# Two transformer layers on one core: dense work to the end, contexts by pairs of heads, whole-height spreading of routing weights

## The chip, the cores and the metric

The kernel runs on one core of one Trainium2 chip. The metric is the device time of one execution in microseconds (us), less is better.

## The reference, cut to what matters

Two layers over x of shape (4, 512, 128), all in float32. Layer 0 adds to x an attention across channels (16 heads) and a mixture of 64 experts with a shared one; layer 1 adds a sparse windowed attention and a dense two-matrix network. This is what the change touches (cut, names shortened):

```
# layer 0, experts: rw is (tokens, 64), the eight chosen weights of each token
expert_out = vmap(lambda g, u, d: (silu(x @ g.T) * (x @ u.T)) @ d.T)(Wg, Wu, Wd)
routed = einsum('eth,te->th', expert_out, rw)

# layer 1, attention: 8 heads of 16 channels, a window of 64 positions
q = relu(einsum('btd,nde->btne', x, enc_q)); v = relu(einsum('btd,nde->btne', x, enc_v))
sig = mean(q, time) + 0.5 * mean(q[:, ::8], time)
metric = softplus(base + 0.1 * (gelu(sig @ w1 + b1) @ w2 + b2))
dist = sqrt(sum((q_window - q)**2 * metric) + 1e-8)      # causal window
w = exp(-dist) of the 32 nearest, divided by their sum
context = sum_k w[k] * v[k]
out = (q * (context + gate * 0.1 * heb)) @ decoder

# layer 1, dense: two ternary matrices
r = relu(x @ Wfc'.T); y = r*r @ Wproj'.T
```

## The kernel before, in words

The four batches (b = 0 to 3) are worked through one after the other. `uses()` assigns eight PSUM banks to uses in order; each engine has parts written as generators, and `ORDER` gives for each engine a string of letters that says which part makes its next step. `weave` plays that string, so the order of the work on each of the five engines is fixed by hand or by a planner outside the file. Each engine runs its instructions in that order; semaphores carry the waits (`filled`, `emptied`, `own`).

**Experts.** The 64 experts and the shared one are cut into 46 tiles of 128 hidden rows for each batch, 184 in all. For a tile TensorE does six fp32r matmuls of 128x512 (`experts()`: high and low halves of weights and tokens into banks G and U), ScalarE the SiLU, VectorE the product with U, VectorE or GpSimd in turn the product with the routing weights `Rb`, and TensorE the down projection (`downs()`), which gathers all 46 tiles of a batch in bank A. ScalarE copies bank A to `mo` at the end of the batch. At most five tiles (`RING`) are under way.

**Routing.** `route(b)` on all engines makes the routing weights, turned into `RW`, and `spread(b, k)` (four for each batch) copies them by one matmul with the selection matrix `sel` to the rows of tile form: lhsT and rhs are rows 32k to 32k+31 of `sel` and `RW`. In the opening, batch 0's transposed tokens go bank X, `xT` (ScalarE), `xH` (ScalarE), `xL` (GpSimd), and the first expert matmul waits for `xL`.

**Layer 1.** `head(b)` (letter h) follows when bank A of the batch is copied: normalisation, the encodings `kp` and `v`, the metric (one column: `met`), the operands of the distances. `vt` is stored to DRAM (`vscratch`), and for each of eight groups g of 64 queries SyncE loads overlapping windows `vw` of 79 rows by four (`windows`, line 409 through `load`); `vw` has two buffers, so the load of group g waits until the context matmuls of group g-2 are done. `distances` (d), `near` (n: square root and exponential on ScalarE), `choose` (k: the 32 nearest by MAX8 and MATCH_REPLACE8 on VectorE), `weights` (q, GpSimd), `turns` (t: transposes `turn`, then the contexts `ctx`, after every second group `dec`), `gather` (g, VectorE) and `adds` (p, GpSimd) follow for each group.

A context is four matmuls of 79x128 by 79x128: every head's values with every head's weights. VectorE multiplies the 128x512 result with the block mask `bd` into `wT`; GpSimd adds the eight blocks in three steps into `cT` (semaphore `added`), adds `hf` and multiplies with `kp` after every second group. For the last group VectorE does all of this.

**Dense part.** `dense(b)` (f) works in four steps i: `ff1` (four matmuls of 128x128x128), ScalarE ReLU and square into `PR`, `ff2` (four matmuls), and VectorE adds the 128x128 result to x. Batch 0's and 1's steps run during the experts of batches 2 and 3, three of batch 2's during the experts of batch 3, and the last of batch 2 and batch 3's own after the last expert. Both `ff1` and `ff2` use bank X0.

The SyncE order is: stores of v and eight window loads for each batch, the output of batch b-1 near batch b's v, and in batch 3 the four outputs of 128 rows between the last window loads.

Helpers stand for most lines: L507 is every matmul (`mm`), L516 the first transposes, L767 the `turn` transposes, L797/L801/L805 VectorE operations, L1280 ScalarE's `activation`, L1285 the load of the logarithm table, L1523 GpSimd's `tensor_tensor`, L409 every DMA. A float32 matmul shows as two instructions in the trace.

Of the kernel before, what the change touches and what calls it, by code (L numbers as in the profile page):

```python
# [12 lines left out]
NT = T // 128  # L13
# [15 lines left out]
LNEXP = "natural_log_exp_and_others"  # L29
TAKEN = 0.0  # L30
# [9 lines left out]
        "vvvvvvvvvsvvvvvvvvvsvvvvvvvvvvsvvvvvsvsvvss",  # L40
    "pe":
        "yyeeyeeemaeemeeeeeaeeeaeayeasessasammmememeeememmmeeeemaueaeeauemmeeaeeeummueyeeyemmyemeeeeeemmmeemm"
        "eeeeememeeeeemmmeeemmeeeeeeemyeemmmseemseemeeemmeseeeeeemmmeeeeemmmseemeeemeeemehyeyeeemmmyeeememhee"
        "mhheeheeheehmehememeemeemmemeeemeeeheheemmmdeeeedmymdamaedamdeeeadtaeeeteeameeammeeemtdmemeeetmdeeee"
        "meeemmeteetmataetataeesesefmmfmteemtfteeeememeeftfeefmmfeetemmfeesmteemseymhtmteeeeeeteeytmeemeytemh"
        "mhmemeeheemmeeeeeehhmheeememhmeeeeeymmmeeeehaemheaedeedemaedeaedadeaatdtmmmmemdteemeemdteeememeemaee"
        "etameeetaeametmmeeeemtseetsefmmfemeeeeefmmemteetmeetemfmfmtfteeeeeefeeefmmteeehestmtmseatmtmameeeamt"
        "aeheeaeeheeahmehmeameemhmheeeeehmmmemeeehaeeeemmmeheeaedeeedeeedemmdedmeeemmtmeadteedeeeetemtmmmdmee"
        "eaemmeeteteetfmmemeetmfeteeeeeememfmfteeeetefteemtetmeefmmmmtmmhtfttfthfhthfhhfhhfffhhfddddfdddttttd"
        "tttttttttttttttt",  # L50
    "dve":
        "cyyyyyyyyyyycyyyelyyyeayeyeyyyyyeylaecyyyeyyayyamammyleemeyaaemeaueuluueuuuamuuuemeemleaemeyyylyemey"
        "emyyyeyylyyyemeemeyyyyyemelyeymeyemleemyeyyyelmeemyeyemleemeemleeeeelmhhemheyhyhhemlyeyyyemyyheoehmh"
        "elehyymyeyelyymyyyeyeyhheemeymhlyemeemlyoakakkokkkkeokkeeakkgakmlaekeemkkkemkklaegmeeamkeeagklkkgkke"
        "amaekkgmkkekyfglyyemekegkekkfyeymfelkmemkkgkfkeegkkeemlhhhgheemelemgyyhhygyyeylyyyyoemeyhyemyeyelmye"
        "hhyyyyyeyememeelhyhmahelehmeaeomkkkkoeakkkakkaokkklgkkeemkkakaekememlageemeklgemkekakkkkemaegekkkmlk"
        "kfeemegeemlgemkekkfgkemlkkgekfekkeefkmelgehmhhhgaeghhaemlgeemaeemhaaoelehhmeaemlahhaeemhelemheemeelm"
        "okkkoeekkkkkkkkeomelkeegkkkmkkmgekaeemlkemgkeakkkemlgkkkeemekekfgklekefmmgekekgkklegmkkemekkkgfhkhhh"
        "gfhhghogfhhfhhfhhokkkokfkkkkkkkkkgokgkkkkkkkkggkkkkgkkkgkkkgkkkgkkkkgkkgggg",
    "act":  # L60
        "xxyxyyexcxeexecxxeeexxaayxsxssyaseeexexexaeexxaaxeeuxexexueuyxexyexexeexxexxeexexxeexexxeeexxeexyexs"
        "xesxeyxexexsxexeexexxesxmexeeexxeyxeyxhexxeexhehxehheexxhxhexxexeeexxexhekxxkenkxeexnkynnknanxkneake"
        "kxgeexxeaexexnnxgxexneexexeeaxxgnanagxeexsesxfeexgfexxyexexfexgefxexesxesmxygeexxexexgyheexxhhexhxee"
# [1681 lines left out]
```

## Time and profile before

| What | us |
|---|---|
| time before, median of three runs | 772.04 (766.23 to 772.14) |
| the profiled execution's own time | 761.87 |
| its span | 760.1 |
| PE busy (matmuls) | 690.4 (91%) |
| VectorE busy | 608.9 (80%) |
| ScalarE busy | 424.2 (56%) |
| GpSimd busy | 423.1 (56%) |

PE is TensorE's matmuls, PEld its weight loads, DVE is VectorE, ACT ScalarE, POOL GpSimd, SPq SyncE's queue. "128\*64" behind a matmul is rows by columns of the weights. Idle time in brackets is the engine's own wait before the row, and what ended it.

### The profile page before, as it was taken

The numbers are of one execution on the slowest core, as the hardware profiler recorded it, in microseconds if no ns is written. First come the engines' busy times: TensorE is split into PE (matmuls) and PEld (weight loads), VectorE is DVE, ScalarE is ACT, GpSimd is POOL, SyncE is SP. The second block draws the span as 40 slices with busy tenths as digits, with TensorE's granted clock in tenths as the row PEclk, the third lists the DMA queues.
The fourth block names the chain that finished last, engine by engine and source line by source line (L and its number), as shares of the span: only waits on it lengthen the run. The fifth ranks groups of instructions, "written<-read, shape, count | busy, mean of one in ns | idle before, by whom it ended". The sixth has DMA issues, their size and how long they took to land.

```text
span 760.1 us, 11266 instructions
## 1 busy us (share of the span) xinstructions
PE 690.4 (91%) x3208; PEld 468.9 (62%) x3208; DVE 608.9 (80%) x2520; ACT 424.2 (56%) x763; POOL 423.1 (56%) x515
## 2 busy tenths in 40 slices
PE   2999999999999899999999899999999999788533
PEld 2656765666656577776555676766566677566433
DVE  3898697659979889989769897975858999759973
ACT  4654543657557665564866665456758564377200
POOL 2165456454656775685628677565745666613540
PEclk9989999999999999999999999999999999997555
DMA  9930000000000000001000000001000000010000
GB/s 285 362 80 1 2 0 0 2 1 16 17 1 5 6 13 18 11 4 34 14 1 6 10 8 15 14 5 31 17 1 2 19 11 13 13 40 11 20 26 17
DMA packets 25722, 21.90 MB, mean 29 GB/s; under 512 B 1920, under 2 KB 23596, under 8 KB 25148
## 3 DMA queue, kind: packets, MB, share of 16 engines
q1 hardware_dynamic: 25660, 21.18, 9.4%
q8 instruction: 26, 0.43, 0.2%
q14 instruction: 36, 0.29, 0.1%
HBM read 18.95 MB, written 2.23 MB: 28 GB/s over the span
## 4 chain that ended last, share of the span: by engine, by line
PE 60%; DVE 21%; ACT 6%; DMA 4%; issue 4%; POOL 3%; SPq 1%; DVEq 0%; POOLq 0%; ACTq 0%
PE bank_X L507 19%; PE bank_U L507 14%; PE bank_A L507 13%; PE bank_G L507 13%; DVE S L797 4%; DVE Wk L1214 4%; DMA vw<-vscratch 4%; DVE m L1211 3%; SPq L409 1%; ACT L1285 1%; PE bank_X L767 1%; DVE Wlo L797 1%; ACT L1280 1%; PE bank_X L516 1%; POOL S L1523 1%
## 5 line engine op out<-in xcount | busy, mean ns | idle before, releaser
L507 PE MATMUL bank_A<-S,WdT 128*128 128x512 f32 x368 | 183.2, 602 | 3.1 <-DVE S L797 1.9
L1523 POOL TENSOR_TENSOR Wlo<-Wgu,Whi 128x256 fp32r<-128x256 f32 x138 | 109.3, 797 | 120.8 <-ACT Whi L1280 120.0
L797 DVE TENSOR_TENSOR S<-S,bank_U 128x512 f32<-128x512 f32 x184 | 123.7, 680 | 52.2 <-PE bank_U L507 30.7
L1280 ACT ACTIVATE S<-bank_G 128x512 f32<-128x512 f32 x184 | 107.8, 595 | 95.4 <-PE bank_G L507 89.0
L1523 POOL TENSOR_TENSOR S<-S,Rb 128x512 f32<-128x512 f32 x88 | 119.1, 1355 | 50.2 <-DVE S L797 49.8
L1280 ACT ACTIVATE Whi<-Wgu 128x256 fp32r<-128x256 f32 x184 | 74.2, 413 | 70.8 <-PE bank_U L507 62.2
L507 PE MATMUL bank_G<-xH,Whi 128*128 128x512 f32 x184 | 93.2, 506 | 2.4 <-ACT S L1280 1.2
L507 PE MATMUL bank_U<-xH,Whi 128*128 128x512 f32 x184 | 91.6, 498 | 3.5 <-DVE S L797 3.5
L507 PEld LDWEIGHTS bank_A<-S,WdT 128*128 128x128 f32 x368 | 66.0, 191 | 45.0 <-issue 26.8
L1214 DVE MATCH_REPLACE8 Wk<-m,Wk 128x79 f32<-128x79 f32 x384 | 82.0, 225 | 0.0
L797 DVE TENSOR_TENSOR S<-S,Rb 128x512 f32<-128x512 f32 x88 | 77.4, 881 | 1.8
L507 PE MATMUL bank_G<-xH,Wlo 128*128 128x512 f32 x184 | 73.1, 397 | 0.0
L507 PE MATMUL bank_G<-xL,Whi 128*128 128x512 f32 x184 | 73.0, 397 | 0.0
L507 PE MATMUL bank_U<-xL,Whi 128*128 128x512 f32 x184 | 73.0, 397 | 0.0
L507 PE MATMUL bank_U<-xH,Wlo 128*128 128x512 f32 x184 | 72.9, 396 | 0.0
L1211 DVE MAX8 m<-Wk 128x8 f32<-128x79 f32 x384 | 63.4, 227 | 0.0
L1523 POOL TENSOR_TENSOR wT<-wT 128x256 f32<-128x256 f32 (+1 forms) x62 | 38.3, 618 | 44.6 <-DVE wT L797 42.0
L507 PEld LDWEIGHTS bank_G<-xH,Whi 128*128 128x128 f32 x184 | 34.9, 190 | 26.0 <-issue 14.8
L1280 ACT ACT_TABLE_LOAD x36 | 46.2, 1283 | 4.4 <-PE bank_A L507 2.9
L507 PEld LDWEIGHTS bank_U<-xH,Whi 128*128 128x128 f32 x184 | 34.9, 190 | 22.3 <-issue 10.1
L507 PEld LDWEIGHTS bank_G<-xL,Whi 128*128 128x128 f32 x184 | 35.0, 190 | 13.4 <-issue 8.8
L1523 POOL TENSOR_TENSOR rr<-kp,cst 128x512 f32<-128x512 f32 x16 | 18.9, 1182 | 43.3 <-PE bank_X L507 30.9
(235 smaller groups left out, 1312.6 us busy)
## 6 DMA issues: line engine op xcount, KB each, us to landing
vw<-vscratch SPq DMA_DIRECT2D x32, 158.0 KB
Wgu<-in_Wgu SPq DMA_DIRECT2D x2, 2048.0 KB, 15.4
xs<-in_x SPq DMA_DIRECT2D x4, 256.0 KB, 7.0
wqk<-in_w_qkv SPq DMA_DIRECT2D x1, 1024.0 KB, 7.6
Wgu<-in_Wgu SPq DMA_DIRECT2D x1, 1024.0 KB, 9.4
vscratch<-mo SPq DMA_DIRECT2D x4, 256.0 KB
out<-xs SPq DMA_DIRECT2D x3, 256.0 KB, 2.3
Wgu<-in_Wgu SPq DMA_DIRECT2D x1, 512.0 KB, 5.4
```

Of the source, the lines that this page charges most:

```text
L409: engine.dma_start(dst, src).then_inc(sems(name), 16)
L507: return engine.matmul(dst, lhsT, rhs, start=start, stop=stop)
L516: p = engine.transpose(t[0:rows, 128 * i:128 * i + 128], src3[:, i, :], ident)
L767: p = engine.transpose(t[0:WK, 128 * i:128 * i + 128], Wk[s][:, i, :], ident)
L797: return engine.tensor_tensor(dst, a, b, op)
L1211: top[i] = own(engine.max(w8[:, i, 8 * r:8 * r + 8], v[:, i, :]))
L1214: p = engine.match_replace(wk[:, i, :], w8[:, i, 8 * r:8 * r + 8], v[:, i, :], TAKEN)
L1280: return engine.activation(dst, src, f, bias=bias, scale=scale, accum_out=acc)
L1285: engine.preload_act_table_set(LNEXP)
L1523: return engine.tensor_tensor(dst, a, b, op)
```

## The change

- `spread`: `sel` becomes four matrices of 128x128, each zero outside its 32 rows (made by VectorE from a new constant `quarter`), and each spread is one matmul over all 128 rows.
- Contexts: each of the four matmuls of a group becomes four of 79x32 by 79x32, one for each pair of heads, into 32 partitions of 32 columns. VectorE takes the diagonal halves by two `scalar_tensor_tensor` operations with the per-partition masks `even` and `odd`, adding `hf` on the way, into `cT`. GpSimd's three additions and the addition of `hf` go; its product with `kp` stays.
- Dense: all of it in the order strings stands after batch 2's experts; only batch 0's first `ff1` is ahead of the last expert. `ff2` goes to bank A (free after the last `mo`), four tiles to a bank, one VectorE addition of 128x512 for each batch in place of four. The output store of a batch waits for that; the stores of batches 0, 1 and 2 stand between batch 3's window loads. `yT` has buffers of its own for batches 0 and 1.
- Metric: `w1` is scaled beforehand (`w1s`), the two means are added by accumulating matmuls; ScalarE takes the absolute value; the chain behind the logarithm has two operations instead of six. For batch 3 the GELU table and the logarithm table are loaded ahead of their use.
- Opening: the logarithm table is loaded first; batch 0's `xH` is read straight from PSUM, and VectorE makes `xL` (and the copy `xT`) from PSUM; the first expert matmul may stand ahead of the gate's.
- All five order strings are new.

The diff, without the order strings and cut to the core:

```diff
-        sel = sb("sel", [128, 128], FR)
+        sel = sb("sel", [128, 4, 128], FR)
...
         for i in range(NT):
             add("X0", "ff1", b, i)
-            add("X0", "ff2", b, i)
+        add("A", "ff2", b)
...
-                sp.wait_ge(empty(bank("ff2", b, j)), nth("ff2", b, j) + 1)
+                sp.wait_ge(empty(bank("ff2", b)), nth("ff2", b) + 1)
...
-                mm(t[:, :], sel[32 * k:32 * k + 32, :], RW[32 * k:32 * k + 32, :]).then_inc(
+                mm(t[:, :], sel[:, k, :], RW[:, :]).then_inc(
...
-                    t = fill("ff2", b, i)
+                    if i == 0:
+                        t2 = fill("ff2", b)
+                        pe.wait_ge("mo", B)
...
-                mm(t[0:64, 0:1], w1[:, :], met[:, 3:4]).then_inc(sems("w1"), 1)
+                mm(t[0:64, 0:1], w1s[:, 0, :], met[:, 0:1], True, False)
                 pe.wait_ge("sig", b + 1)
+                mm(t[0:64, 0:1], w1s[:, 1, :], met[:, 1:2], False, True).then_inc(sems("w1"), 1)
...
                     for i in range(GT):
-                        p = mm(t[:, 128 * i:128 * i + 128], vw[s][:, i, :], wT[s][0:WK, 128 * i:128 * i + 128])
+                        for j in range(0, 128, 32):
+                            p = mm(t[j:j + 32, 32 * i:32 * i + 32], vw[s][:, i, j:j + 32],
+                                   wT[s][0:WK, 128 * i + j:128 * i + j + 32])
...
+                if b == 0:
+                    yield
+                    dve.wait_ge("xH", 1)
+                    t = filled("xT", 0)
+                    tt(xLs[0][:, :], t[:, :], xHs[0][:, :].bitcast(F), ALU.subtract).then_inc(sems("xL0"), 1)
+                    emptied(engine.tensor_copy(xTs[0][:, :], t[:, :]), "xT", 0)
...
+                yield
+                dve.wait_ge("ff2_tile", NT * (b + 1))
+                after_adds(b)
+                latest[b] = emptied(tt(x, x, ps("ff2", b)[:, :], ALU.add), "ff2", b)
...
-                    a = emptied(tt(w3, t[:, :].rearrange("p (a n) -> p a n", a=GT),
-                                   bd.unsqueeze(1).to_broadcast([128, GT, 128]), ALU.mult), "ctx", b, g)
+                    dve.wait_ge(*own(stt(c3, t4[:, :, 0, :], K("even"), h3, ALU.mult, ALU.add)))
+                    a = emptied(stt(c3, t4[:, :, 1, :], K("odd"), c3, ALU.mult, ALU.add), "ctx", b, g)
...
+            logarithms()
...
+                if b == B - 1:
+                    table[0] = GELU
+                    engine.preload_act_table_set(GELU)
...
+                a = act(met[:, 5:6], t[:, 8:9], ACT.Abs, bias=mb[:, 2:3], scale=0.1)
...
-                    po.wait_ge(*own(tt(w4[:, :, 0:4, :], w4[:, :, 0:4, :], w4[:, :, 4:8, :], ALU.add)))
-                    po.wait_ge(*own(tt(w4[:, :, 0:2, :], w4[:, :, 0:2, :], w4[:, :, 2:4, :], ALU.add)))
-                    tt(cT[:, t0:t0 + GT * TQ].rearrange("p (a t) -> p a t", a=GT), w4[:, :, 0, :], w4[:, :, 1, :],
-                       ALU.add).then_inc(sems("added"), 1)
```

The orders around the last expert (dn3.45 is the last down projection; ff0.1:2 is `ff2` of batch 0, step 1; letters that repeat are left out). Before, TensorE: ff2.0 to ff2.2 before it, then `dn3.45 mo3 ff2.3:1 turn2.7 ff2.3:2 ctx2.7 y3 ff3.0:1 enc3 v3 ff3.0:2 met ... ff3.3:1 dist3.0 ... dist3.6 turn3.0 ctx3.0 turn3.1 ctx3.1 dist3.7`. After: `ff0.0:1 ... dn3.45 mo3 ff0.0:2 turn2.7 ff0.1:1 ctx2.7 ... y3 ff0.2:2 enc3 ff0.3:1 v3 ... pq3 ff1.2:2 ff1.3:1 dist3.0 ff1.3:2 ff2.0:1 dist3.1 ... dist3.4 turn3.0 dist3.5 ff2.2:2 ctx3.0 dist3.6 ff2.3:1 dist3.7 turn3.1 ff2.3:2 ff3.0:1 ctx3.1 ff3.0:2 ... ff3.2:1 turn3.2 ...`, the last step ff3.3:2 behind ctx3.3. SyncE after (v = window load of batch 3): `v-store, out0, v0, v1, out1, v2, out2, v3, v4, v5, v6, out3.0, out3.1, v7, out3.2, out3.3`; before: `v-store, out2, v0 to v4, out3.0, v5, out3.1, v6, v7, out3.2, out3.3`.

## Rows read from the trace of the kernel before

**Rows 1.** Busy time by stretch: from:to, length, engines busy (count), PEclk, DMA share, GB/s
```profile
100.00:200.00 100.00, 98.71 (x364) 63.50 (x363) 78.25 (x177) 55.44 (x107) 56.47 (x63) 1.00 0.02 5
...
600.00:640.00 40.00, 39.25 (x197) 28.81 (x196) 38.55 (x188) 24.29 (x44) 28.22 (x35) 1.00 0.05 12
...
660.00:680.00 20.00, 15.94 (x97) 12.20 (x95) 11.12 (x35) 11.63 (x21) 5.02 (x8) 0.91 0.14 34
...
700.00:720.00 20.00, 12.15 (x45) 9.68 (x44) 19.63 (x148) 5.84 (x12) 10.42 (x17) 0.50 0.08 20
720.00:740.00 20.00, 6.58 (x27) 5.62 (x26) 14.94 (x110) 1.19 (x2) 8.78 (x16) 0.50 0.10 26
```

**Rows 2.** Timeline of TensorE and SyncE in the tail: start, us, what, idle before
```profile
696.56 2.08 PE L507 MATMUL bank_U<-wT,vw 79*128 79x128 f32 x8 [0.68 <-ACT wT L1280]
...
698.66 0.22 SPq L409 DMA_DIRECT2D vw<-vscratch  x1
...
726.47 2.05 PE L507 MATMUL bank_U<-wT,vw 79*128 79x128 f32 x8 [1.17 <-DMA vw<-vscratch]
735.15 2.05 PE L507 MATMUL bank_U<-wT,vw 79*128 79x128 f32 x8 [5.78 <-DMA vw<-vscratch]
...
752.37 2.05 PE L507 MATMUL bank_U<-wT,vw 79*128 79x128 f32 x8 [5.60 <-DMA vw<-vscratch]
```

**Rows 3.** The chain that ended last, two pieces: start, us, what
```profile
621.13 0.89 PE bank_X L507 x8
...
756.98 0.78 PE bank_X L507 x2
```

**Rows 4.** Timeline of TensorE around one spread
```profile
324.56 1.02 PE L507 MATMUL bank_A<-S,WdT 128*128 128x512 f32 x2
325.51 0.49 PE L507 MATMUL bank_X<-RW,sel 32*128 32x512 f32 x1
325.93 0.50 PE L507 MATMUL bank_U<-xH,Whi 128*128 128x512 f32 x1
326.27 0.39 PE L507 MATMUL bank_U<-xL,Whi 128*128 128x512 f32 x1
326.50 0.40 PE L507 MATMUL bank_U<-xH,Wlo 128*128 128x512 f32 x1
```

**Rows 5.** Timeline of TensorE around layer 0's small matmuls
```profile
280.30 1.09 PE L507 MATMUL bank_X<-wout,z 64*64 64x128 f32 x16
281.32 0.50 PE L507 MATMUL bank_G<-xH,Whi 128*128 128x512 f32 x1
...
529.86 0.40 PE L507 MATMUL bank_U<-xH,Wlo 128*128 128x512 f32 x1
530.18 1.15 PE L507 MATMUL bank_X<-GWk,wqk 128*64 128x64 f32 x32
531.26 1.13 PE L507 MATMUL bank_A<-S,WdT 128*128 128x512 f32 x2
```

**Rows 6.** Groups by line and form: count, busy us, mean ns, idle before
```profile
L1523 POOL TENSOR_TENSOR wT<-wT 128x256 f32<-128x256 f32 x31 | 24.1, 779 | 42.1 <-DVE wT L797 42.0
...
L797 DVE TENSOR_TENSOR wT<-bank_X,cst 128x512 f32<-128x512 f32 x24 | 16.3, 681 | 1.7 <-PE bank_X L507 1.7
```

**Rows 7.** Timeline of the opening
```profile
8.56 1.28 ACT L1285 ACT_TABLE_LOAD   x1
...
14.49 1.97 PE L507 MATMUL bank_X<-gateT,xT 128*128 128x64 f32 x8 [0.69 <-ACT xT L1280]
15.18 1.27 POOL L1523 TENSOR_TENSOR xL<-xT,xH 128x512 fp32r<-128x512 f32 x1 [3.20 <-ACT xH L1280]
...
16.50 0.79 PE L507 MATMUL bank_G<-xH,Whi 128*128 128x512 f32 x1
```

**Rows 8.** Timeline of batch 3's metric on VectorE and ScalarE
```profile
667.40 1.11 DVE L805 SCALAR_TENSOR_TENSOR met<-met 128x1 f32<-128x1 f32 x1
...
672.41 1.28 ACT L1285 ACT_TABLE_LOAD   x1
...
675.21 1.62 DVE L797 TENSOR_TENSOR met<-met 128x1 f32<-128x1 f32 x3 [0.35 <-ACT met L1280]
```

More of the change, by code:

```diff
@@ L29 @@
 LNEXP = "natural_log_exp_and_others"
+GELU = "gelu_and_others"
 TAKEN = 0.0
@@ L75 @@
 for _n, _w in (("ident", 128), ("bd", 128), ("tri", 64), ("neglo", 1), ("ones", 128), ("heads", NH + 128), ("pick", 128),
-               ("eps8", 1), ("sel", 128)):
+               ("eps8", 1), ("even", 1), ("odd", 1), ("sel", 128), ("quarter", 4)):
     CONST[_n] = (_at, _w)
@@ L100, in constants @@
     put("sel", (p[:, None] % 16 == p[None, :] // 8) * 1.0)
+    put("quarter", p[:, None] // 32 == np.arange(4)[None, :])
+    put("even", p[:, None] // HD % 2 == 0)
+    put("odd", p[:, None] // HD % 2 == 1)
     put("eps8", np.full((128, 1), 1e-8))
@@ L191, in uses @@
             add("X0", "sp", b + 1, 1)
-            dense(b - 1)
             add("X0", "sp", b + 1, 2)
-    dense(B - 2)
-    dense(B - 1)
+    for b in range(B):
+        dense(b)
     for b in range(B):
@@ L262, in program @@
         w1 = sb("w1", [128, 64])
+        w1s = sb("w1s", [128, 2, 64])
         b1 = sb("b1", [64, 1])
@@ L310, in program @@
         vt = yn
-        yT = sb("yT", [128, T])
+        yTs = [sb(f"yT{i}", [128, T]) for i in range(2)]
         kp = sb("kp", [128, PADK + T])
@@ L400, in yT_of @@
         def yT_of(b):
-            return xTs[0] if b == B - 2 else yT
+            return yTs[b] if b < 2 else xTs[b % 2]
         def sync_engine(engine):
@@ L668, in dense @@
                     for k in range(4):
-                        p = mm(t[:, 0:128], r[:, 128 * k:128 * k + 128], WpT[:, k, :], k == 0, k == 3)
-                    p.then_inc(sems(full(bank("ff2", b, i))), 1)
+                        p = mm(t2[:, 128 * i:128 * i + 128], r[:, 128 * k:128 * k + 128], WpT[:, k, :], k == 0, k == 3)
+                    p.then_inc(sems("ff2_tile"), 1)
             def routes():
@@ L895, in route @@
                     dve.wait_ge("ld_c", 16)
-                    engine.tensor_copy(sel[:, :], K("sel")).then_inc(sems("sel"), 1)
+                    for k in range(4):
+                        a = ts(sel[:, k, :], K("sel"), K("quarter")[:, k:k + 1], None, ALU.mult)
+                    a.then_inc(sems("sel"), 1)
                 yield
@@ L1099, in setup @@
                 stt(mb[:, 2:3], mb[:, 0:1], 0.1, mb[:, 1:2], ALU.mult, ALU.add).then_inc(sems("mb"), 1)
+                ts(w1s[:, 0, :], w1[:, :], 1.0 / T, None, ALU.mult)
+                ts(w1s[:, 1, :], w1[:, :], 0.5 / (T // 8), None, ALU.mult).then_inc(sems("w1s"), 1)
             def dense(b):
-                x = xb(b)
-                for i in range(NT):
-                    yield
-                    t = filled("ff2", b, i)
-                    after_adds(b)
-                    latest[b] = emptied(tt(x[:, i, :], x[:, i, :], t[:, 0:128], ALU.add), "ff2", b, i)
+                x = xb(b).rearrange("p a c -> p (a c)")
+                yield
+                dve.wait_ge("ff2_tile", NT * (b + 1))
+                after_adds(b)
+                latest[b] = emptied(tt(x, x, ps("ff2", b)[:, :], ALU.add), "ff2", b)
             def head(b):
@@ L1121, in head @@
                 dve.wait_ge(empty(bank("enc", b)), nth("enc", b) + 1)
-                a = own(engine.tensor_reduce(met[:, 1:2], kp[:, PADK::8], AX, ALU.add))
-                dve.wait_ge(*own(ts(met[:, 2:3], met[:, 0:1], 1.0 / T, None, ALU.mult)))
-                stt(met[:, 3:4], met[:, 1:2], 0.5 / (T // 8), met[:, 2:3], ALU.mult, ALU.add).then_inc(sems("sig"), 1)
+                engine.tensor_reduce(met[:, 1:2], kp[:, PADK::8], AX, ALU.add).then_inc(sems("sig"), 1)
                 yield
@@ L1448, in head @@
                 act(hb[:, :], ps("met", b)[0:64, 0:1], ACT.Gelu, bias=b1[:, 0:1]).then_inc(sems("hb"), 1)
+                if b == B - 1:
+                    logarithms()
                 yield
+                t = filled("met", b)
+                sc_.wait_ge("mb", 1)
+                a = act(met[:, 5:6], t[:, 8:9], ACT.Abs, bias=mb[:, 2:3], scale=0.1)
+                a.then_inc(sems("mabs"), 1)
                 sc_.wait_ge("mabs", b + 1)
-                act(met[:, 6:7], met[:, 5:6], ACT.Exp).then_inc(sems("mexp"), 1)
+                act(met[:, 6:7], met[:, 5:6], ACT.Exp, scale=-1.0).then_inc(sems("mexp"), 1)
+                yield
                 sc_.wait_ge(empty(bank("bdq", b)), nth("bdq", b) + 1)
```

164 lines of the change are left out of this document (79 added, 85 removed).

## Prediction, made before the changed kernel was run

> **What bounds the kernel now.** I read first the busy time by stretch [rows 1]. Up to the last expert (some 655 us) the matmuls fill the span: 98.71 of 100 us, and 39.25 of 40 late on. The same rows show the clock at 1.00, that is 2.4 GHz. VectorE is at 78% there, late at 96% (38.55 of 40), GpSimd and ScalarE far below. So this part is as long as TensorE's instruction stream, and what leaves that stream shortens the kernel one to one, as long as VectorE follows. After 660 TensorE is no longer full (15.94 of 20), and from 700 on it is at 12.15, then 6.58 of 20 with the clock at 0.50 (1.2 GHz), while VectorE falls from 19.63 to 14.94.
>
> Next the timeline of the tail [rows 2]. The first context of batch 3 begins at 696.56 and takes 2.08 us; the load of the next window buffer is issued at 698.66, the moment it ends. The following contexts wait for "DMA vw": 726.47, 735.15, 752.37 (a fourth, at 743.87, is alike). They stand 8.5 to 8.7 us apart, and six loads of 8.6 plus 2.1 us for the first to start give 698.66 + 53.7 = 752.4, where the last context stands. So the transfers run end to end, and the tail from 698.66 on is six window loads, whatever the engines do. VectorE idles in that time. The DMA share in [rows 1] is only 0.08 to 0.10, some one and a half engines of 16: these loads are serial, the path is not full.
>
> The kernel is thus a TensorE part, a chain (head of batch 3, some 25 us, and first choice, 16 us), and a DMA part. The sum is made against the profiled execution, 761.87 us with a span of 760.1; the other runs' median, 772.04, is 1.3% more.
>
> **Dense part.** Eight instructions of one `ff1` or `ff2` step take 0.89 us in the chain [rows 3]; a pair 1.8. Before, 11 pairs stand ahead of the last expert (four each of batches 0 and 1, three of 2), after it half a pair: 10.5 x 1.8 = **-18.9 us** in the full part. They move behind it, where TensorE is not full. In the head, 7.5 pairs stand where 4.5 did: 3 x 1.8 = 5.4 us more on an engine that idles 4.1 of 20 us in that stretch [rows 1], so at most some 1.3 us of it should show, and that in return for waits it fills. The other 8.5 pairs stand among the distances and up to the fourth context: at 2.4 GHz 15 us, at 1.2 GHz 31, in the time in which TensorE is idle for the window loads. What covers them is those loads; if it were gone they would cost up to 31. On VectorE 16 additions become four. What is late next is the store of a batch's output: SyncE issues `out1` ahead of window load 2 and `out2` ahead of load 3, and each waits for a whole batch's `ff2`. `out1`'s addition stands ahead of the first choice, so it is in time. `out2`'s stands behind the third choice, some 19 us after the first begins, and load 3 is not needed by the queue until load 2 is through (8.6 us after context 0, at about the same time): taken at 0, up to 6 us if it slips. Three stores of 256 KB now share the DMA engines with the loads. 16 engines carry one, so each adds its sixteenth to the busy one, 16 KB against the 158 KB of 8.6 us: 0.9 us each, and one or two of them fall after context 0: **+0.9**.
>
> **Spreads.** A spread costs more than its matmul, since it is over 32 rows and its neighbours over 128 [rows 4]. Two down projections (0.86) from 324.56 would end at 325.42; the spread begins at 325.51, the next starts 0.42 later and the one after 0.34, where whole-height fp32r matmuls of 512 columns stand 0.23 apart (326.27 to 326.50). Over 128 rows this is 0.23 and no switch: 0.09 + 0.19 + 0.11 = 0.39 saved, by 16: **-6.2 us**. The bounds are 0 and -8. Four makings of `sel` on VectorE instead of one delay the opening by some 0.5 us, behind ScalarE's weight copies.
>
> **Contexts.** This is the cost of the change. A group has now 32 instructions (16 matmuls, two each) of 32 columns by 32 in place of eight of 128, which take 0.89 like a dense step, with the same loads [rows 3]. No row has this form. The nearest is the similarity product, 128 rows by 64 columns, 64 streamed, the two column halves in turn [rows 5]: 32 in 531.26 - 530.18 = 1.08, 0.034 each. Entering a column form costs 0.09 (530.18 against 529.86 + 0.23), leaving it 0.11 as in [rows 4]. So 1.28 against 0.89, +0.39, and 23 groups stand ahead of the last expert: **+9.0 us**. Bounds: half the columns could halve the time (0.54 + 0.2, -3.5 us in all); or each costs what the 64x64 form does [rows 5], 281.32 - 280.30 = 1.02 for 16, 0.064 each: 2.25, +31 us. I take 0.034 because that row has the same full height and column tiles; its neighbour streams 128 columns, which alone explain 0.053.
>
> Behind them VectorE's 0.681 us mask [rows 6] becomes two operations on 128x64, 0.2 to 0.3 each, -0.2 by group; GpSimd loses an addition of 0.779 us [rows 6] and two smaller ones by group. GpSimd is not the bound, so I cost this at nothing in the full part. Only at the very end is it on the path: from the last context's end (754.42) to the last decode, 756.98 [rows 2, 3], six VectorE operations take 2.5 us, and three would take 1.0: **-1.4 us**.
>
> The Trainium skill speaks against this edit in two places. "TensorE: Matmul & The Clock Gate", section "Wait — 56ns, not 53.3ns?", has the sequencer spend about 62 ns on each MATMUL when the array work is shorter than that; by it a group would take some 2.0 us and the edit would cost about 25 us. Its section "Part 3: Packing small matmuls — row/col tiling" lets a weight load run beside a matmul only in another row group, and the four column tiles share all rows. The similarity rows at 0.034 us for a load and a matmul contradict both, so I don't follow them, but they are the first rival.
>
> **Opening.** The table load at 8.56 (1.28 us) goes ahead of the data, and `xT`, `xH`, `xL` become `xH` from PSUM (0.6) and a VectorE subtraction (0.7, against GpSimd's 1.27) [rows 7]: the first expert matmul comes some 2.5 us earlier than 16.50. But the gate's matmuls (1.97) filled that wait, and stand now behind it. I take **-2.0** (bounds -0.5 and -3.5).
>
> **Head, choice.** In the metric a 1.11 us operation beside GpSimd goes, a table load of 1.28 us is made ahead, and four operations after the logarithm go, of which three took 1.62 [rows 8]: 3.5 to 4 us. Against it stand dense steps on ScalarE (1.25 us each) between the GELU, the exponential and the logarithm, and the 1.3 us of TensorE from above. Net **-2.0** (bounds -5 and +6). The first turn of batch 3 stands no longer behind the distances of group 6: **-0.7**.
>
> **Sum.** -18.9 - 6.2 + 9.0 - 2.0 = -18.1 up to the last expert; -2.0 - 0.7 - 1.4 + 0.9 = -3.2 behind it: -21.3. 761.87 - 21.3 = 740.6, a ratio of 0.972, and on the median 772.04 this is **750.5 us**.
>
> **Rivals.**
>
> *Small context matmuls cost more by the piece.* For: no row shows 32x32 tiles, and [rows 5] has 0.064 for 64x64. Against: the 0.034 row, the nearest in height. 23 groups x 32 = 736 pieces, so each 0.01 us above 0.034 costs 7.4 us; from 0.063 the gain is gone. At 0.064 the kernel stands at 772. If each piece costs what a 128-column load and matmul does, 0.112 (0.89 by 8), it is 57 us more: 808. This is the case that ends slower.
>
> *The dense part is given back behind the experts.* The head becomes TensorE's own length, or its ScalarE steps delay the metric; the output store holds SyncE ahead of a window load. For: 15.94 of 20 are already busy, and the clock halves behind 696, which doubles a pair to 3.6 us. Then the head's -2.0 becomes +3.4 and a late load 3 adds 3 to 6: about 760.
>
> *The full part doesn't follow.* VectorE at 96% in 600 to 640 takes over as the bound in the last batch, and half of the dense gain stays off the path: +10, 761. Against it: VectorE's own work shrinks too, and over the whole part it is near 80%.
>
> **Chances.** Forecast 0.68; context pieces at 0.063 or more 0.07 (0.02 of it near no change, 0.05 slower); given back 0.15; doesn't follow 0.10. A measurement of this kernel can tell about 1% from no change. Below 764.3: 0.68, and most of the second and third rivals, 0.86 in all; within 1% 0.09; slower 0.05. The range is 734 to 765: the low end has contexts for nothing, the opening and head at their best; the high end takes in both middle rivals. The low side also holds that the later runs may stand as near the profile as 741.
>
> **What would show it.** After: the spreads 0.23 us before their successor, as 128x512; contexts x32, 1.08 to 1.3 us from start to next; the last down projection some 18 us earlier; GpSimd's `wT` additions gone; contexts of batch 3 still 8.6 us apart waiting for the window DMA, and the stretch from the first context of batch 3 to the end at 61 us (63.5 before, from its start). Wrong would be: contexts of 2 us or more at the full clock; gaps between TensorE's rows in the last batch's experts with VectorE named; window loads further apart than 9 us with an output issue between them; or a head longer than 25 us from `mo` to the first distance.

## The result, and the profile after

| | before | changed |
|---|---|---|
| median of the runs beside each other, four each | 769.65 us | 735.36 us |
| ratio, 95% interval | | 0.957 (0.951 to 0.963) |
| profiled execution | 761.87 us | 739.74 us |
| its span | 760.1 us | 737.9 us |
| last `mo` copy, and the time from it to the end | 653.09, 107.01 | 634.40, 103.50 |

Between the profiled executions it is 22.1 us, between the medians 34. Executions of both kernels gather at two levels that go with the mean granted clock (before some 763 us at 0.947 and some 771 at 0.933, changed some 735 at 0.970 and some 740 at 0.962), so the profiled pair sets before's shorter level against the changed kernel's longer one, and like against like the change is worth 28 us (763 to 735) or 31 (771 to 740). In a later set (`e5_after_again`) it is 740.06 against 763.06, 0.970 (0.968 to 0.971). The argument below is from the profiles.

Busy time of the kernel before, by the stretches between its `mo` copies (one copy a batch; the last row is the tail). Columns as in [rows 1]:

```profile
158.73:326.53 167.80, 165.11 (x782) 110.40 (x780) 146.68 (x617) 103.87 (x188) 104.82 (x125) 1.00 0.04 10
326.53:497.39 170.86, 165.78 (x800) 113.78 (x798) 143.44 (x601) 104.91 (x187) 108.27 (x133) 0.99 0.04 12
497.39:653.09 155.70, 153.69 (x735) 102.54 (x733) 125.56 (x535) 96.42 (x168) 97.34 (x113) 1.00 0.05 12
653.09:760.10 107.01, 64.51 (x326) 51.04 (x326) 75.51 (x486) 39.44 (x77) 36.27 (x58) 0.68 0.08 22
```

The same of the changed kernel:

```profile
16.00:159.20 143.20, 135.36 (x555) 89.53 (x556) 114.18 (x263) 72.11 (x133) 71.93 (x77) 0.96 0.20 66
159.20:321.55 162.35, 157.62 (x877) 101.93 (x876) 138.15 (x584) 102.40 (x187) 92.56 (x103) 1.00 0.04 11
321.55:482.19 160.64, 157.13 (x924) 100.70 (x922) 141.48 (x633) 96.77 (x176) 96.25 (x105) 0.98 0.04 11
482.19:634.40 152.21, 148.70 (x902) 94.93 (x903) 124.65 (x552) 89.45 (x162) 83.43 (x86) 0.99 0.04 12
634.40:737.90 103.50, 65.59 (x732) 54.20 (x731) 71.88 (x470) 49.98 (x97) 19.61 (x25) 0.83 0.10 27
```

The stretches shrink by 5.5, 10.2 and 3.5 us. TensorE's busy time shrinks by 21.1 us in the three, and its idle time grows from 9.8 to 11.8. The first stretch, with all of the opening's edits, is no shorter: the first `mo` copy came at 158.73 and comes at 159.20. Keep this stretch apart in all that follows: a run whose edit isn't in it can still differ from before there by 2 us, with the clock. So each part is also given between its own first and last `mo` copies, which are 494.4 us apart before and 475.2 in the changed kernel (-19.2).

Now the two small matmul forms that the prediction priced. TensorE's timeline of the changed kernel, answering to [rows 4] and [rows 5]:

```profile
145.46 0.39 PE L512 MATMUL bank_G<-xH,Wlo 128*128 128x512 f32 x1
145.69 0.40 PE L512 MATMUL bank_X<-RW,sel 128*128 128x512 f32 x1
145.93 1.02 PE L512 MATMUL bank_A<-S,WdT 128*128 128x512 f32 x2
...
256.71 0.40 PE L512 MATMUL bank_U<-xH,Wlo 128*128 128x512 f32 x1
257.04 0.46 PE L512 MATMUL bank_X<-wT,vw 79*32 79x32 f32 x32
257.43 1.13 PE L512 MATMUL bank_A<-S,WdT 128*128 128x512 f32 x2
```

The spread stands 0.24 from its successor, where 0.23 was forecast. The context group does not: from its start to the next instruction 0.39 us, not 1.08. With 0.10 to enter the form (257.04 against 256.71 + 0.23) and 0.11 to leave it (the down projections behind it show 1.13 where they show 1.02 at 145.93), a group takes 0.6 us where the old one took 0.89 [rows 3]. The new form is cheaper than what it replaces.

TensorE in the tail of the changed kernel, answering to [rows 2]:

```profile
678.25 0.46 PE L512 MATMUL bank_U<-wT,vw 79*32 79x32 f32 x32
...
707.20 0.66 PE L512 MATMUL bank_U<-wT,vw 79*32 79x32 f32 x32 [1.03 <-DMA vw<-vscratch]
715.75 0.66 PE L512 MATMUL bank_U<-wT,vw 79*32 79x32 f32 x32 [5.72 <-DMA vw<-vscratch]
724.25 0.66 PE L512 MATMUL bank_U<-wT,vw 79*32 79x32 f32 x32 [3.74 <-DMA vw<-vscratch]
733.09 0.66 PE L512 MATMUL bank_U<-wT,vw 79*32 79x32 f32 x32 [7.10 <-DMA vw<-vscratch]
```

Still 8.5 us apart, still on the window loads: the tail from the first context on is the same six transfers.

### The profile page after: what moved, and what is told of

Read it like the earlier page. It is cut to its first block, busy times and chain, and to the rows that moved or that the text cites. A ratio compares the mean times of both kernels' runs of the same rounds, so it can differ in the third digit from the quotient of the medians.

```text
span 737.9 us, 12696 instructions
## 1 busy us (share of the span) xinstructions
PE 667.7 (90%) x3984; PEld 443.9 (60%) x3984; DVE 596.5 (81%) x2527; ACT 414.0 (56%) x759; POOL 367.5 (50%) x406
## 4 chain that ended last, share of the span: by engine, by line
PE 48%; DVE 37%; issue 4%; POOL 4%; ACT 3%; DMA 2%; SPq 1%; DVEq 0%; ACTq 0%; POOLq 0%
PE bank_X L512 13%; PE bank_A L512 12%; PE bank_G L512 11%; PE bank_U L512 10%; DVE S L809 9%; DVE Wk L1233 9%; DVE m L1230 6%; DVE GWk L809 2%; DMA vw<-vscratch 2%; SPq L414 1%; DVE rr L809 1%; POOL S L1550 1%; DVE hg L817 1%; DVE Wlo L809 1%; PE bank_X L521 1%
## 5 line engine op out<-in xcount | busy, mean ns | idle before, releaser
L512 PE MATMUL bank_A<-S,WdT 128*128 128x512 f32 x368 | 188.0, 613 | 2.1 <-POOL S L1550 1.2
L1550 POOL TENSOR_TENSOR S<-S,Rb 128x512 f32<-128x512 f32 x88 | 117.4, 1335 | 94.7 <-DVE S L809 94.3
L809 DVE TENSOR_TENSOR S<-S,bank_U 128x512 f32<-128x512 f32 x184 | 124.0, 679 | 43.4 <-PE bank_U L512 27.2
L512 PE MATMUL bank_U<-xH,Whi 128*128 128x512 f32 x184 | 96.2, 523 | 9.1 <-DVE S L809 8.8
L512 PE MATMUL bank_G<-xH,Whi 128*128 128x512 f32 x184 | 98.3, 534 | 3.9 <-POOL Wlo L1550 2.1
L512 PEld LDWEIGHTS bank_U<-xH,Whi 128*128 128x128 f32 x184 | 35.3, 192 | 34.1 <-DVE S L809 17.7
L512 PEld LDWEIGHTS bank_U<-xL,Whi 128*128 128x128 f32 x184 | 35.3, 192 | 14.3 <-issue 10.3
L1550 POOL TENSOR_TENSOR Wk<-Ed,Wk 128x316 f32<-128x316 f32 x31 | 29.5, 953 | 23.4 <-DVE Wk L1233 23.2
L512 PEld LDWEIGHTS bank_G<-xH,Wlo 128*128 128x128 f32 x184 | 35.2, 191 | 8.5
```

The source lines that it names most:

```text
L512: return engine.matmul(dst, lhsT, rhs, start=start, stop=stop)
L809: return engine.tensor_tensor(dst, a, b, op)
L1550: return engine.tensor_tensor(dst, a, b, op)
```

## The experiments

Before's place of the last `mo` copy and the rest of its span are 653.09 and 107.01; the changed kernel's are 634.40 and 103.50.

**Contexts.** First the changed kernel with its context matmuls at the old width:

```diff
-for j in range(0, 128, 32):
-    p = mm(t[j:j+32, 32*i:32*i+32], vw[s][:, i, j:j+32],
-           wT[s][0:WK, 128*i+j:128*i+j+32])
+p = mm(t[:, 128*i:128*i+128], vw[s][:, i, :], wT[s][0:WK, 128*i:128*i+128])
```

> The changed kernel with the four context matmuls of a group at their old width (79x128 by 79x128); VectorE still reads 128 columns of the bank, which are then those of the wrong heads, so the output lacks the right contexts. In the changed kernel's trace 32 pieces of 32 columns start and are done in 0.39 us, with 0.1 us of switching on either side. Theory A (TensorE's stream bounds the part ahead of the last expert): a group costs 0.89 instead of 0.59 us, 23 groups ahead of the last expert give +6.9 us, the last context at the slow clock +1.5: about 743 to 745 against 735.4. Theory B (the form of the matmul is hidden, the edit's gain is in what VectorE and GpSimd no longer do): under +2 us, 735 to 737.

Then the kernel before with the contexts by pairs of heads and nothing else of the change (the short matmuls as above, two VectorE operations on 64 columns, no additions on GpSimd; orders as before without those additions).

> The kernel before with the contexts by pairs of heads alone (matmuls, VectorE's two operations with hf, GpSimd's additions gone), orders otherwise as before. Theory A with the measured 0.59 us a group: -0.30 x 23 = -6.9 us ahead of the last expert and -2.9 us behind the last context, together -9 to -10 (ratio about 0.987). Theory as predicted (0.034 us for a piece): +9 us ahead of the last expert, -1.4 at the end, ratio 1.010. Theory B (the order string decides, small gains are lost again): only the end's -2.9, ratio 0.996.

Measured: e1 741.94 us, 0.971 (0.966 to 0.976) of before. e2 755.21 us, 0.989 (0.983 to 0.994). So the part that was forecast to cost 9 us and give back 1.4 gains 8.8 alone by its ratio, and the rival with pieces of 0.06 us or more is dead. The profile of e2 splits it: the last `mo` copy comes at 649.65 (-3.4), and 102.75 follow (-4.3). The -3.4 has two parts. The first `mo` copy comes 2.4 us late (161.12, with the clock at 0.96 up to there where before had 0.98), though batch 0's experts have no contexts among them and the orders there are before's; between the first and the last copy e2 gains 5.8 us of the 6.9 that theory A had. Three rows of its tail show the 4.3:

```profile
693.50 0.66 PE L506 MATMUL bank_U<-wT,vw 79*32 79x32 f32 x32 [0.68 <-ACT wT L1275]
...
747.47 0.66 PE L506 MATMUL bank_U<-wT,vw 79*32 79x32 f32 x32 [6.77 <-DMA vw<-vscratch]
749.26 0.76 PE L506 MATMUL bank_X<-dec,hg 128*128 128x128 f32 x2 [1.14 <-DVE hg L798]
```

At 1.2 GHz a context is 0.66 us where it was 2.05 [rows 2]. The first one, shorter by 1.4, lets the chain of loads begin 1.4 us sooner; the last is shorter by 1.4; and behind it VectorE's additions are 1.4 shorter, the one item of the three that was priced. First context to last is 53.97 us (693.50 to 747.47), where before had 55.81 [rows 2].

In e1 the reverse was worth less than its rows say. Its groups cost 0.3 us more each, 6.9 over 23, yet its last `mo` copy stands at 635.18, 0.8 behind the changed kernel's (0.1 between the first and the last copy), and beside the control below (0.970) its ratio differs by 0.001. That was the first sign that TensorE's stream does not pass its savings on one to one. It also leaves open what made the gain of e2: e1 puts back TensorE's part of the edit alone, while e2 takes work off VectorE and GpSimd as well.

**Spreads.** The kernel before with `sel` in four masked copies and the spread's matmul over 128 rows:

```diff
-mm(t[:, :], sel[32*k:32*k+32, :], RW[32*k:32*k+32, :])
+mm(t[:, :], sel[:, k, :], RW[:, :])
```

> The kernel before with the spreads over all 128 rows alone. Theory A: 16 x 0.39 = -6.2 us (ratio 0.992). Theory B (the spreads stand where TensorE waits anyway, or VectorE follows late): 0 to -2 us. The opening may lose 0.5 us by the three more makings of sel.

Measured: 764.46 us, 1.002 (0.999 to 1.006): no gain, 6.2 were forecast. The profile:

```profile
159.37:326.58 167.21, 164.25 (x782) 110.66 (x780) 146.60 (x617) 103.84 (x189) 104.83 (x125) 1.00 0.04 10
326.58:499.53 172.95, 170.44 (x799) 117.30 (x798) 146.12 (x601) 104.71 (x186) 107.22 (x133) 0.95 0.04 12
499.53:654.74 155.21, 153.23 (x735) 102.73 (x733) 125.48 (x535) 96.30 (x168) 97.30 (x113) 1.00 0.05 12
```

Four spreads a batch should take 1.6 us out of each stretch. Two stretches are 0.6 and 0.5 us shorter than before's; the one between them lost 2.1, with the clock at 0.95 where before had 0.99. A third of the sum arrived in the two, and one dip of the clock outweighed it. What began that dip isn't in TensorE's rows ahead of it. From 390 on they are those of before within 0.02 us, up to this one, in e3 and then in before:

```profile
403.06 2.00 PE L508 MATMUL bank_X<-mk,rr 128*128 128x79 f32 x8
403.07 1.12 PE L507 MATMUL bank_X<-mk,rr 128*128 128x79 f32 x8
```

From there the clock of e3 is 0.51 and 0.50 up to 418, that of before 1.00. So a run of one profile can't tell a spread's gain in that stretch from the clock, and the spreads stay at 1.1 us shown out of the two others.

**Dense part alone.** The kernel before with the whole dense part behind the last expert, by the changed kernel's code (`ff2` of a batch in one bank, one addition of 512 columns) and its order from the last `mo` copy on:

```diff
-            dense(b - 1)
...
-    dense(B - 2)
-    dense(B - 1)
+    for b in range(B):
+        dense(b)
```

> The kernel before with its dense part alone moved behind the last expert, as the change has it (one addition of 512 columns for a batch; its order behind the last mo copy is the changed kernel's, the rest of the orders is that of before with the dense letters taken out). Theory A (the prediction's pricing: 10.5 pairs at 1.8 us leave TensorE's full stream, hidden behind the metric at the end): 744 to 747 us, ratio 0.973 to 0.979, all of the gain ahead of the last mo copy (653.1 to about 635), tail within 2 us of 107. Rival B (part is given back: with other stages late, TensorE idles in the places the pairs had, and the two levels of the granted clock eat some): 750 to 756 us, ratio 0.983 to 0.991. Rival C (the twelve added pairs lengthen the tail by more than 5 us): mo copies as in A, tail above 112.

> The kernel before with the dense part last, as in the run before with it, but in ScalarE's order behind the last expert the metric's exponential stands behind the first ReLU of the second batch and its logarithm ahead of the next one. There the logarithm stood behind a ReLU, VectorE waited 6.7 us for it and TensorE, idle for 3 us, fell to 1.2 GHz while dense pairs had to run. Theory A (the 13 us that the tail had grown are that order, not the twelve pairs' own time): mo copies as there (160.4, 327.2, 494.8, 649.4), tail 108 to 113 instead of 120.0, ratio to the kernel before 0.995 to 1.000. Rival B (the pairs themselves lengthen the tail): tail 117 or more, ratio 1.005 or more.

Measured: e8 770.69 us, 1.010 (1.008 to 1.012), slower than before. e9 765.58 us, 1.002 (0.999 to 1.005). Ahead of the first `mo` copy the edit changes nothing. What the first order did, in TensorE's and VectorE's timelines of e8:

```profile
674.55 2.05 PE L483 MATMUL bank_A<-WpT,PR 128*128 128x128 f32 x8 [3.07 <-ACT PR L1257]
676.38 1.92 PE L483 MATMUL bank_X<-yT,WfT 128*128 128x128 f32 x8
679.65 2.08 PE L483 MATMUL bank_A<-WpT,PR 128*128 128x128 f32 x8 [1.35 <-ACT PR L1257]
...
679.72 0.55 DVE L775 TENSOR_TENSOR met<-met 128x1 f32<-128x1 f32 x3 [6.69 <-ACT met L1257]
```

TensorE stood 3.07 us, the clock fell to 0.76 in 671 to 676 and 0.50 in the five us after, a dense step then took 1.9 us instead of 0.9, and the metric's logarithm stood behind a ReLU that waited for those steps: VectorE waited 6.69 us. Two operations moved in ScalarE's order gave back 6.3 us (tail 119.96 in e8, 113.67 in e9). The same place in TensorE's timeline of e9:

```profile
676.06 1.16 PE L483 MATMUL bank_A<-WpT,PR 128*128 128x128 f32 x8 [1.82 <-ACT PR L1257]
677.05 1.06 PE L483 MATMUL bank_X<-yT,WfT 128*128 128x128 f32 x8
```

That was half of the tail's growth of 13.0 us, and not all of what theory A claimed (108 to 113): 6.7 us remain. From the `mo` copy to the first distance matmul it is 31.1 us (650.33 to 681.44) where before had 27.2. This is the forecast's 1.3, at 3.9.

The larger miss is ahead of the tail. The last `mo` copy comes at 650.33 instead of 653.09, the first at 161.02 instead of 158.73 (clock 0.96 against 0.98, the same instructions in the same orders). Between them it is 489.3 us instead of 494.4: **5.1 us for eleven pairs priced at 18.9.** The stretches of e9:

```profile
161.02:328.45 167.43, 160.50 (x718) 103.65 (x716) 146.47 (x613) 99.51 (x181) 104.85 (x125) 0.99 0.04 10
328.45:495.62 167.17, 160.16 (x736) 106.68 (x734) 141.31 (x596) 100.75 (x178) 107.27 (x132) 0.98 0.04 10
495.62:650.33 154.71, 149.68 (x687) 96.81 (x685) 126.28 (x534) 92.98 (x162) 98.40 (x114) 1.00 0.04 11
```

64, 64 and 48 instructions left the stream (so batch 0's and 1's dense steps had stood among the experts of batches 1 and 2, not 2 and 3 as the description of the kernel says), at sixteen a pair eleven pairs, and 14.2 us of TensorE's busy time. But its idle time rose from 2.7, 5.1 and 2.0 us to 6.9, 7.0 and 5.0: 9.2 of the 14.2 us became waiting. Of the 4.7 us between 18.9 and 14.2 some may be the clock (0.99 and 0.98 in the first two stretches, 1.00 and 0.99 before); the rest wasn't taken apart.

**Who it waits for.** The next two runs lighten VectorE and GpSimd, whose lateness is the suspect:

```diff
-tt(s[:, :], s[:, :], Rb[k][:, :], ALU.mult)
+tt(s[:, 0:8], s[:, 0:8], Rb[k][:, 0:8], ALU.mult)
```

> The kernel before with the multiplications by the routing weights (22 of 46 products in a batch, on VectorE and GpSimd) cut from 512 columns to 8: this leaves the weighting of the other columns out. It takes some 14 us of VectorE's and more of GpSimd's time out of each batch. Theory A (TensorE's stream is the bound up to the last expert, as the prediction said; idle 4.0, 2.7, 5.1 and 2.0 us): the last mo copy comes at most 4 us earlier (653.1 to 649 or later), ratio 0.994 or more. Rival B (the other engines' lateness is already in that idle time and in the granted clock): 8 us or more earlier.

> The dense part last, mended as in the first of these runs, and the weight multiplications cut to 8 columns as in the second (it leaves the same weighting out). Theory A (with the pairs gone from the stream, products that VectorE and GpSimd deliver late are what TensorE waits for, so that of 20 us of pairs only 3.7 us were gained): the idle time of the three segments falls from 18.0 us to 9 or less, and the last mo copy comes 8 to 15 us ahead of that of the first run (649.4 to 634 to 641), more than twice what the same cut gives the kernel before. Rival B (it is the clock or the order of the banks, and not the load of the other engines): the cut gives what it gives the kernel before, within 3 us.

Measured: e10 755.7 us (six of its ten runs, 748.76 to 758.42), 0.989 (0.984 to 0.993), last `mo` copy at 647.08; e11 746.35 us, 0.974 (0.965 to 0.983), last `mo` copy at 632.26. The profiled execution of e10 took 762.95 us. Its tail is 7.1 us longer than before's, with the clock at 0.62 where before had 0.68, so only what lies ahead of it is used. There the clock is nearly that of before:

```profile
157.93:323.03 165.10, 164.28 (x782) 110.72 (x780) 129.13 (x617) 103.89 (x189) 75.56 (x125) 1.00 0.04 11
323.03:492.87 169.84, 166.43 (x800) 114.30 (x798) 125.61 (x601) 105.09 (x186) 79.55 (x133) 0.98 0.04 12
492.87:647.08 154.21, 152.80 (x735) 102.95 (x733) 111.80 (x537) 96.44 (x168) 68.47 (x113) 1.00 0.05 13
```

The last `mo` copy of e10 is 6.0 us earlier than before's, between the two expectations. That of e11 is 18.1 earlier than e9's, but 6.2 of it are in the first stretch (154.78 against 161.02), where neither has a dense step. Between the first and the last copy the cut gives the kernel before 5.2 us and the kernel with the dense part last 11.8, over twice as much. Read the other way, moving the dense part is worth 5.1 us with the other engines as they are and 11.7 with them lightened. The idle time of TensorE in the three stretches falls from 19.0 us in e9 to 9.5 (2.6, 4.0 and 3.0); theory A had 9 or less. The cut also shortens each tile's way through its buffers, of which there are five (`RING`), and it lightens two engines at once: which of these counts wasn't taken apart. The stretches of e11:

```profile
154.78:315.44 160.66, 158.04 (x718) 103.51 (x716) 127.98 (x613) 99.50 (x180) 75.81 (x125) 1.00 0.04 11
315.44:480.61 165.17, 161.22 (x736) 108.21 (x734) 123.71 (x594) 100.40 (x179) 78.20 (x131) 0.97 0.04 10
480.61:632.26 151.65, 148.69 (x687) 97.35 (x685) 111.23 (x534) 92.85 (x163) 69.85 (x115) 1.00 0.04 11
```

**Both large parts.**

> The kernel before with the dense part last (mended) and the contexts by pairs of heads, the two large parts together; alone, the one brought the last mo copy from 653.1 to 649.4 and the other to 649.7. Theory A (the two gains add up, and the rest of the change's 18.7 us up to there came from its new orders): last mo copy at 645 to 648, ratio to the kernel before 0.984 to 0.990. Rival B (the contexts' part takes work off VectorE's and GpSimd's way, a product of 512 columns and three additions for a group, which is what the dense part's gain needs): more than the sum, last mo copy at 642 or earlier, ratio below 0.981.

Measured: 760.84 us, 0.994 (0.990 to 0.998); last `mo` copy at 643.04, tail 114.76. The gain ahead of the tail is 10.0 us where the two alone make 6.2, between the two expectations. But the first stretch, where none of the three edits has a part, is 2.3, 2.4 and 1.4 us longer than before's in e9, e2 and e12, and the sum of two counts it twice. Between the first and the last `mo` copy e12 gains 11.4 us and the two alone 5.1 and 5.8, 10.9 together: they add up, as theory A had it, and don't help each other. And the head is 34.7 us now (643.04 to 677.73), and by the ratio both parts together give 4.7 us, less than the contexts alone. Some 20 us of the change's gain are in neither, 8.6 ahead of the tail and 11.3 in it. What is left for it are the shorter metric and opening, the spreads and the new orders; these weren't taken apart. The waits of VectorE from 160 to 630 point to the orders. Before:

```profile
DVE S L797 <- ACT S L1280: 18.4, 14, 4.9
```

and in the changed kernel, where e12 still has 17.7:

```profile
DVE S L809 <- ACT S L1293: 6.1, 11, 1.1
```

VectorE's queue stood 18.4 us behind SiLUs that ScalarE had not delivered, and what TensorE wanted from it stood behind them. The new orders take 12 us of that away; VectorE's waits for TensorE's bank U rise from 18.2 to 22.5 in the same time. That these 12 us are the missing gain is argued, not shown: in e11 VectorE waits 20.2 us for the same SiLUs, and its last `mo` copy is earlier than the changed kernel's (632.26 against 634.40), so the length of this wait alone doesn't tell what it costs. No run has the new orders alone.

**Opening and window loads**, with the changed kernel as its own control:

> The changed kernel as it is, on the chip and in the call of the next three, so that they are compared with it and not with runs of another session. Both theories: its ratio to the kernel before lies at 0.961 to 0.969 if the kernel before runs at its quicker level of 762 to 765 us here (735.4 / 763), and at 0.957 only if that one runs at its slower level of 770 to 773 us, as it did in most of its runs beside the first measurement of the change. Then the part of the 34 us that the two profiled spans do not show (22.2) is the level of the kernel before, not the change.

> The changed kernel with two instructions moved forward in VectorE's order of the opening: the product for expert step 0.3 to ahead of the routing comparison, that for 0.4 to ahead of the four MAX8. Theory A (the opening's expected gain was given back by this order, since TensorE stood 2.96 us at 30.4 for the bank that the product for 0.3 frees): the hole closes, the first mo copy comes 2 to 3.5 us earlier (159.2 to some 156.5), the granted clock behind it no longer dips at 31 to 51, ratio to the changed kernel 0.993 to 0.997. Rival B (the hole is only moved: the routing chain ends about 1.3 us later, the spreads and the attention behind it wait instead): within 0.2% of the changed kernel, first mo copy within 0.7 us.

> The changed kernel with window loads of 80 rows instead of 79 (the last row is not used; it is read from a row more in DRAM). Theory A (in the tail the loads of 79 rows run on one DMA engine, 8.6 us each end to end, and set its length): 80 rows go over 16 engines, a load lands 2 to 4 us after its issue, contexts of batch 3 no longer wait for it, and the tail becomes VectorE's choices: 8 to 11 us less, about 726. Theory B (the tail is set by the choices and the chain behind them, the waits for the loads only fill what would be waited for anyway): under 2 us less, 733 to 735.

> The changed kernel with both the windows of 80 rows (as in the run before with them) and the two products moved forward. If the two gains are independent, as one lies in the first 160 us and the other behind the last mo copy at 634: about 730.3 - 2.5 = 728 us, ratio to the changed kernel 0.988 to 0.991. If the early order gives nothing: that of the 80 rows alone, 0.993.

Measured: e5 740.06 us, 0.970 of before (0.968 to 0.971); e6 736.90, 0.966 (0.963 to 0.968); e4 730.31, 0.954 (0.947 to 0.961); e7 728.04, 0.955 (0.952 to 0.957). The opening's gain was real and was spent: the first expert matmul came at 13.81 instead of 16.50 [rows 7], but VectorE's new order ran the routing chain ahead of one product (TensorE's timeline, then VectorE's):

```profile
33.33 0.80 PE L512 MATMUL bank_U<-xH,Whi 128*128 128x512 f32 x1 [2.96 <-DVE S L809]
...
32.59 1.28 DVE L809 TENSOR_TENSOR S<-S,bank_U 128x512 f32<-128x512 f32 x2
```

With the two products moved forward (e6) TensorE's matmuls run on to 32.4. Then it waits 1.67 us for VectorE's `Wlo` (up to 34.03) and 1.70 for its `xn` (up to 36.67), and the clock of 36 to 41 is 0.50:

```profile
31.00:36.00 5.00, 2.30 (x9) 1.05 (x7) 4.86 (x33) 3.76 (x8) 1.01 (x2) 0.92 0.96 350
36.00:41.00 5.00, 4.33 (x11) 2.92 (x12) 4.22 (x15) 0.99 (x3) 0.56 (x1) 0.50 0.92 227
```

So the hole of 2.96 us became two of 3.37 together: it was moved, as the rival said. The first `mo` copy still came 1.7 us earlier than the control's (157.76 against 159.49), less than theory A's 2 and more than the rival's 0.7, and on top of the wider windows nothing can be told (0.955 in e7, 0.954 in e4).

The window loads are the tail. With one row more a window (80 instead of 79; the store wrote one row more and nothing else changed):

```diff
-vw = [sb(f"vw{i}", [WK, GT, 128]) for i in range(2)]
+vw = [sb(f"vw{i}", [WK + 1, GT, 128]) for i in range(2)]
...
-return bass.AP(rows.tensor, rows.offset, [[128, WK], [TQ * 128, GT], [1, 128]])
+return bass.AP(rows.tensor, rows.offset, [[128, WK + 1], [TQ * 128, GT], [1, 128]])
```

the DMA view of 678 to 728 gives a median of 2.4 us from issue to landing, and the last contexts of e4 wait for no load:

```profile
vw<-vscratch SPq DMA_DIRECT2D x6, 160.0 KB, 2.4
```

```profile
706.85 0.66 PE L513 MATMUL bank_U<-wT,vw 79*32 79x32 f32 x32 [0.68 <-ACT wT L1294]
...
723.97 0.66 PE L513 MATMUL bank_U<-wT,vw 79*32 79x32 f32 x32 [0.68 <-ACT wT L1294]
```

Its last `mo` copy is at 634.40 as in the changed kernel, and 94.40 us follow instead of 103.50. VectorE waits for little but itself then (2.9 us from 678 on, 11.8 in the changed kernel), so its choices are what is left. e4 and e7 are the shortest of all these kernels; the wider windows are to be kept.

## Why the prediction was right, and where it was wrong

The forecast was -21.3 us on the profiled execution; it is -22.1. Ahead of the last `mo` copy -18.1 was forecast and -18.7 came; behind it -3.2, and -3.5 came. Almost none of the terms is right by itself. The total holds because a large cost that was not there stands against gains that did not arrive, and that is luck. So is the match to a microsecond: it is with this pair of profiled executions, and like against like, as above, the change is worth 28 to 31 us.

- *"As long as TensorE's instruction stream, and what leaves that stream shortens the kernel one to one, as long as VectorE follows."* This is the step that failed. The condition was named, looked at as a busy share of 78% and 96%, and set aside at a chance of 0.10. A share says nothing of the order: an engine with an in-order queue can be late at each step with a fifth of its time free. Taken alone, between the first and the last `mo` copy, the dense part gave 5.1 of 18.9 us and the spreads 1.1 of 3.1 in the two stretches where the clock is like; with VectorE and GpSimd lightened the dense part gave 11.7. The contexts, which take work off those two engines as well, gave 5.8 of 6.9. The rival "the full part doesn't follow" was the true mechanism of a large part of this, with half of the dense gain lost as it said and more. In the whole change -19.2 came between the copies. Why it gives 7.7 us more than e12 there isn't shown; new orders that let the others follow are the likely reason.
- *Contexts, +9.0.* The mis-sized term. 32 pieces were priced at 0.034 us by the similarity rows, and take 0.39 together, 0.012 each. That is below the lower bound that was given, a half of the similarity's time. On TensorE's stream the term is -6.9 (23 x 0.3; in both traces 22 groups stand ahead of the last down projection, which makes it -6.6), 16 from the forecast; on the kernel before it gave -5.8 between the first and the last `mo` copy. The warning that was cited from the Trainium skill ("TensorE: Matmul & The Clock Gate", section "Wait — 56ns, not 53.3ns?") is out by more: 32 MATMULs and their 32 loads start within 0.39 us, 12 ns for a load and its MATMUL. The section gives its 62 ns for matmuls decoded by the sequencer's software, with the hardware's decoding off; the prediction left this condition out, and no run here shows which of the two was on. Not to follow it was right, on the evidence of rows.
- *Behind the last context, -1.4.* 7.7 us before (752.37 to 760.1), 4.8 now (733.09 to 737.9). The VectorE part is the 1.4 forecast; a context that is 1.4 us shorter at 1.2 GHz was left out, there and at the start of the chain of loads.
- *Spreads, -6.2.* The size on TensorE was right, 0.24 to the successor. It did not arrive alone.
- *Opening, -2.0.* The first expert matmul did come 2.7 us earlier; 2.96 went back at 30.4 behind VectorE's new order. It moved the first `mo` copy by +0.5.
- *Head, -2.0,* and *first turn, -0.7.* The head, to the first distance matmul, went from 27.2 to 26.4 us. It was counted with 7.5 pairs where the order and the trace have 7, so that 2.5 pairs, 4.5 us, came in and not 5.4. They cost 3.9 in e9, not 1.3, and the shorter metric and its order must have gained more than was counted. From the last `mo` copy to the first context it is 43.9 us, where before had 43.5: +0.4 for the -2.7 of the two terms. The tail's total holds by the term before this one. A head longer than 25 us was named as a sign of being wrong; it had been longer in the kernel before, too.
- *Stores, +0.9,* and *six window loads end to end:* right. From the issue of the first load to the last context it was 53.7 us and is 54.3 (678.78 to 733.09). The first context to the end was forecast at 61 us and is 59.65; the loads still set the contexts' places, as the 80-row run shows by taking them away. But "VectorE idles in that time" holds late only: from 700 to 720 it was busy 19.63 of 20 us [rows 1], and so the tail without the loads' waits is 9.1 us shorter and not more.
- For the median 750.5 was forecast and 735.4 came, near the low end of the range, and -34 us where the scaled sum had -21.5.

## What to carry to other kernels

A gain on the fullest engine is worth only what the engines that feed it in order can keep up with (here 5.1 us of 18.9, and 11.7 with less work on them). Their busy share doesn't tell this; take the block out, see how much of it turns into waits, and lighten the others as a test. Compare stretch by stretch, and first one that the edit can't touch: 2 us of difference there are not the edit's. And where a transfer sets the pace, look first at its shape: one row more was worth 9 us of span, about twice the 4.7 us that the two largest parts of the change gave together in e12.

## What the runs showed of the hardware

- Matmuls of 32 columns by 32 in four column tiles, 79 rows deep, start 0.012 us apart on average (32 in the 0.39 us from 257.04), each with its weight load, although all four share the same rows. Changing into and out of the form costs 0.10 and 0.11 us, once for a group of 32. At 1.2 GHz the group took 0.66 us, and the eight of 128 columns 2.05.
- A load of 79 rows takes 8.5 us for 158 KB and one of 80 rows 2.4 us for 160 KB. The Trainium skill's page "DMA: Bandwidth & Descriptors", section "Why a DMA increments its semaphore by 16 and not by 1", splits a transfer over the largest number up to 16 that divides its slowest dimension: 1 for 79 and 16 for 80. The trace agrees: some 19 GB/s over the tail of the changed kernel while loads run, and a landing 3.5 times sooner.
- Waits of TensorE were followed by stretches at 1.2 GHz: 3.07 us in e8, then 0.50 in 676 to 681; 1.67 and 1.70 us in e6, then 0.50 in 36 to 41. There a late engine was paid for twice. But the clock also fell for some 15 us in e3 behind rows that are those of before, where it did not fall. What began that dip is open.
